# Two groups of indirect DMAs on GpSimd's queue change places in a mixture-of-experts kernel

## The reference

```python
h = layernorm(x).reshape(-1, 128)                 # 2048 tokens
probs = softmax(h @ router_weight.T)              # 8 experts
topk_probs, selected = top_k(probs, 2)            # each token goes to two experts
capacity = ceil(1.25 * 2 * 2048 / 8)              # 640 rows to an expert
expert_inputs = rows of h, gathered per expert    # [8, 640, 128]
pre  = expert_inputs @ ff_pre_act_weight.T        # [8, 640, 512]
gate = expert_inputs @ gate_weight.T
expert_out = (pre * silu(gate)) @ ff_post_act_weight.T
out = x + scatter_add(expert_out * kept_weight)   # back to the tokens' rows
```

## Time and profile before

| what | us |
|---|---|
| median of 3 timed runs (lowest, highest) | 385.89 (384.17, 385.9) |
| span of the profiled execution, first to last instruction | 410.6 |
| PE busy | 305.2 |
| VectorE busy | 290.1 |
| GpSimd busy | 211.5 |
| ScalarE busy | 144.4 |

### The profile page before, as it was taken

One profiled execution on the slowest core, in us unless ns is written; L12 is line 12 of the kernel. 1 busy time (PEld: TensorE's weight loads), 2 busy tenths in 40 slices (PEclk: granted clock), 3 DMA queues, 4 the chain that ended last, 5 costly groups with the idle time before them and its releaser, 6 DMA issues.

```text
span 410.6 us, 5169 instructions
## 1 busy us (share of the span) xinstructions
PE 305.2 (74%) x1465; PEld 212.9 (52%) x1465; DVE 290.1 (71%) x615; ACT 144.4 (35%) x285; POOL 211.5 (52%) x145
## 2 busy tenths in 40 slices
PE   5969996776798669766591866969695959597940
PEld 4635342333344335333261555959594949497940
DVE  5954999999999999999978843646363636362500
ACT  2535963223533353344042003333332323233320
POOL 0632455974455435543714062174848484848664
PEclk9965996887888878988786798978797979798995
DMA  6040024254000000000002011144443333323332
GB/s 186 2 102 0 0 52 102 62 140 164 14 13 0 26 26 0 0 26 26 0 27 77 1 41 26 32 92 76 72 85 59 79 62 86 55 48 43 29 26 25
DMA packets 20756, 20.31 MB, mean 49 GB/s; under 512 B 2624, under 2 KB 14848, under 8 KB 20736
## 3 DMA queue, kind: packets, MB, share of 16 engines
q1 hardware_dynamic: 13184, 14.63, 12.4%
q0 software_dynamic: 7040, 5.25, 10.3%
q10 hardware_dynamic: 512, 0.19, 0.3%
HBM read 10.82 MB, written 5.05 MB: 39 GB/s over the span
## 4 chain that ended last, share of the span: by engine, by line
PE 38%; DVE 25%; issue 13%; another core or an unknown queue 9%; POOL 7%; ACT 4%; DMA 1%; DVEq 1%; POOLq 1%; ACTq 0%
PE psum L1481 10%; DVE ring L518 8%; PE psum L1460 5%; PE psum L1315 5%; DVE ring L509 5%; PE psum L1462 5%; PE psum L1461 4%; POOL ring L1130 4%; PE psum L1298 2%; DVE sm L543 2%; POOL out L1197 2%; DVE xn L457 1%; POOL parts L1119 1%; PE psum L1295 1%
## 5 line engine op out<-in xcount | busy, mean ns | idle before, releaser
L1130 POOL TENSOR_TENSOR ring<-ring,cbc 128x1024 f32<-128x1024 f32 x31 | 74.9, 2416 | 85.7 <-DVE ring L518 85.7
L518 DVE TENSOR_TENSOR_SCAN ring<-ring 128x1024 f32<-128x1024 f32 x32 | 102.6, 3210 | 0.0
L1315 PE MATMUL psum<-ring,cst 128*128 128x512 f32 x128 | 76.4, 729 | 15.4 <-POOL ring L1130 15.3
L1298 PE MATMUL psum<-stack,sel_r 128*128 (+1 forms) x120 | 55.8, 572 | 25.4 <-DVE ring L509 24.7
L1197 POOL DMA_INDIRECT out<-ring,sid x40 | 62.9, 1572 | 16.9 <-issue 11.0
L1180 POOL DMA_INDIRECT ring<-rows,gid x40 | 38.7, 968 | 63.4 <-DVE gid L780 39.5
L817 DVE TENSOR_TENSOR ring<-psum,ring 128x320 f32<-128x320 f32 x64 | 31.4, 491 | 56.0 <-ACT ring L1048 30.6
L1460 PE MATMUL psum<-stack 128*128 128x320 f32 x128 | 47.6, 372 | 27.2 <-issue 16.4
L935 ACT ACTIVATE ring<-psum,nega 128x510 f32<-128x510 f32 x64 | 41.7, 681 | 46.1 <-PE psum L1298 44.4
L1048 ACT ACTIVATE ring<-psum 128x320 f32<-128x320 f32 x64 | 27.9, 438 | 78.7 <-PE psum L1462 50.8
L1298 PEld LDWEIGHTS psum<-stack,sel_r 128*128 128x128 f32 x120 | 25.1, 224 | 53.4 <-DVE ring L509 33.6
(11 more groups left out here) (180 smaller groups left out, 342.4 us busy)
## 6 DMA issues: line engine op xcount, KB each, us to landing
stack<-parts SPq DMA_DIRECT2D x16, 256.0 KB, 3.8
win_s<-in_wg SPq DMA_DIRECT2D x8, 256.0 KB
win_s<-in_w SPq DMA_DIRECT2D x8, 256.0 KB
w_s<-in_w SPq DMA_DIRECT2D x8, 256.0 KB
xt<-in_x SPq DMA_DIRECT2D x4, 256.0 KB, 4.7
out<-xt SPq DMA_DIRECT2D x4, 256.0 KB, 2.3
rows<-xn SPq DMA_DIRECT2D x4, 256.0 KB, 2.3
ring<-rows,gid POOLq DMA_INDIRECT x40
```

Of the source, the lines that this page charges most:

```text
L518: v.tensor_tensor_scan(hh[:, s].rearrange("p a b -> p (a b)"), da[:, s].rearrange("p a b -> p (a b)"), uu[:, s].rearrange("p a b -> p (a b ...
L1130: g.tensor_tensor(hc[:, s], hh[:, s], cb, ALU.mult).then_inc(s_product, 1)
L1298: ins = mm(bank(to + k), sel, stack[:, half, kind, bass.ts(c, CH)], start=True, stop=True)
L1315: ins = mm(bank(YB), wred[:, o:o + D], hc[:, s, k, :], start=(grp == 0), stop=(grp == NG - 1))
```

## The change

In GpSimd's `expert`, the block that waits for the row numbers of expert `e+2` and issues its five gathers moves from ahead of the five scatters of expert `e` to behind them. Nothing is added or removed.

```diff
             def expert(e, b, more=True):
 
-                if more:
-                    gather_ready(e + 2, b)
-                    for q in range(NQ):
-                        gather(b, q)
                 pool.wait_ge(s_scatter_ids, 2 * e + 2)
                 for q in range(NQ):
                     pool.wait_ge(s_weighed, NQ * e + q + 1)
...
                     g.indirect_dma_start(out=out, out_offset=bass.IndirectOffsetOnAxis(ap=sid[:, b, q:q + 1], axis=0),
                                          in_=ye[:, b, q, :], in_offset=None, compute_op=ALU.add
                                          ).then_inc(s_scattered, 16)
+                if more:
+                    gather_ready(e + 2, b)
+                    for q in range(NQ):
+                        gather(b, q)
```

## The result

The kernel after takes 444.85 us in the median of four timed runs (444.15 to 447.76), the kernel before 385.89 (384.17 to 387.4). The ratio is 1.151, with a 95% interval of 1.146 to 1.156: 59 us slower, where 57 were forecast (443.0 us).

A forecast was written before the change was run, and what follows sets the result against it. GpSimd's issuing was taken to bound the timed kernel at 15.8 us a round; the new chain of 25.4 us a round adds 34.5 + 22.6 = 57.1 to 385.9, giving 443.0 us (429 to 450; 8 in 10: 418 to 455).

The forecast's parts named there:

- the 24.7 us: Profiled span of the kernel before, 410.6 us, less its timed median, 385.89; forecast held timed GpSimd lacks 22.6 us of waits.
- the profiled pace: Rival: timed rounds are as long as the profiled ones, so only 34.5 us count: 420 us (407 to 428), chance 0.17.
- The chain: GpSimd and PE work that overlapped becomes one sequence from expert e's first scatter to e+1's: 23.1 to 26.6 us, middle 25.4.
- last issue to its transpose: From the end of the fifth gather's issue on GpSimd to PE's transpose: 2.68 us, with 1.61 as the other end.
- last transpose to the next `up`: On PE, one transpose, two `down` tiles, table, last `down` tile: 3.29 us at full clock, 5.1 at 0.50.
- `up` to the first scatter: From the start of PE's `up` to GpSimd's first scatter: 2.69 us, some 0.7 longer at the low clock.
- The row-number wait: GpSimd's wait before the gathers of expert e+2: taken at nothing behind the scatters, at most 5.1 us.
- The landing: Fifth gather, from the start of its issue to its transpose: 3.63 us by the row, 2.15 by the skill's estimate.
- The clock: PE's granted clock in the burst after waiting for gathers: 1.00 or 0.50, rounds 24.13 or 26.6 us, middle 25.4 taken.
- The low end of 5.1: Last transpose to next `up` at clock 0.50: 3.29 us lengthened by the 1.55 ratio of tile pairs, 2.77 against 1.79.
- The sum: Expert 6's scatters 34.5 us later than profiled, plus 22.6 us of waits: 57.1 on 385.9 gives 443.0 us.
- Issues shorter than their rows: Rival: GpSimd's issues take less time than traced, round 18.0 us, 376 us in all; not slower has chance 0.04.

## Why the prediction was right

**The reading of the long profile.** The choice that the 24.7 us belong to one profiled execution, and that GpSimd's issuing bounds the timed rounds, was argued from a sum. The second profile of the kernel before shows it: no waits, a span of 382.3. Had the profiled pace been taken as real, the forecast would have been 420, too low by 25 us. What delayed that one execution stays open. Its silus waited for matmuls that had been issued, and neither the second profile of before nor the profile after shows such "remote" waits.

**The chain.** The terms of a round, forecast and measured in the six rounds of the trace after:

| term | forecast, us | measured, us |
|---|---|---|
| five scatters | 9.11 | 9.07 to 9.12 |
| gap to the gathers | 0.30 | 0.30 to 0.31 |
| five gathers | 6.06 | 6.05 to 6.07 |
| last issue to its transpose | 2.68 (1.61) | 1.89 to 2.63 |
| last transpose to the next `up` | 3.29 to 5.1 | 4.56 to 5.84 |
| `up` to the first scatter | 2.69 to 3.4 | 2.77 to 2.96 |
| round | 25.4 | 26.0 in the mean |

The row-number wait was costed at nothing, and no gather of the rounds waits for it. The landing was a little quicker than the row taken: 329.63 - 326.79 = 2.84 us from the start of the last gather's issue to its transpose in the round shown, and 3.4 to 3.6 in the others, against 3.63. The Trainium skill ("DMA: Bandwidth & Descriptors", Anatomy of one DMA) led to an estimate of 2.15; the rows decide, and the estimate is low.

**The clock** is the term that was mis-sized. The forecast took the middle between a burst at the full and at the low level, 4.2 us for the stretch from the last transpose to the next `up`. It took 5.2 in the mean: in the round shown nearly all of the burst is at the low level (0.51) behind 11 us with PE busy for 2. The low end of 5.1 was itself too short for such a round (5.7). It came from a ratio of 1.55 for two tiles, read from a pair that began at 0.50 and ended after the clock was back at 1.00; here the pair takes 3.41 against 1.79, 1.9 times as long. Landing and `up` took back some 0.4 us a round. The slow start of the burst is as the Trainium skill ("TensorE: Matmul & The Clock Gate", HAM oscillation) has it, that a burst behind each DMA wait starts slow; by that rule the forecast was 450 us, since it also put the first matmuls of `up` at the low level. They are not: `up` to the first scatter takes 2.77 to 2.96 us.

**The sum.** First scatter of expert 0: forecast 4.3 us earlier than before, 267.1 against 271.40. In the trace after and the second one of before it is 260.07 against 264.22, so 4.15 earlier. Six rounds after: 152.0 forecast, 155.96 measured. The way from expert 0's first scatter to expert 6's before: forecast 113.2 - 22.6 = 90.6, measured 356.45 - 264.22 = 92.2. So -4.15 + 155.96 - 92.2 = 59.6 us, and the spans differ by 442.1 - 382.3 = 59.8. Two errors, of 4.0 us in the rounds after and 1.6 in those before, offset each other and left the forecast 2 us low: the mechanism was right, and part of the closeness is luck.

**The rivals.** The profiled pace fell with the second profile. Issues shorter than their rows fell too: rows of 1.56 and 0.95 us with their gaps add up to 15.8 us a round, and the kernel before runs at 16.0 in its second profile, with GpSimd issuing without a pause.

## What to carry to other kernels

A queue that serves two consumers one behind the other ties them together: before an issue is moved behind a wait, follow what that wait needs back to the moved issue, and if the path closes on itself, the cost is the sum of the loop less what bounded the round before. Here the price was then paid per issue that stood ahead, not once, and could be read off durations that the trace already had. And when a profiled span is longer than the timed median, the profile's waits may not be those of the timed runs; a second profile settled it here.

## What was not expected

The scatters' landing takes longer than their issue and is mostly hidden here. With one scatter ahead of the gathers, 4.53 us passed from the end of the last scatter's issue to the first scatter of the next expert, against an issue of 1.56. In the kernel before it also holds VectorE, which waits for scatters to land before it writes new row numbers (L788), as the waits of the second profile show:

```profile
DVE tk L788 <- DMA out<-ring,sid: 23.1, 6, 5.4
```

That they did not set the rounds is read from GpSimd's having no pause beside them, and from the 4.95 us or more that the weighed tiles were early. Where a round has fewer issues, the landing does show, in the kernel before too. Expert 6 has no gathers ahead of its scatters, and its first scatter waits 2.57 us:

```profile
356.45 1.56 POOL L1197 DMA_INDIRECT out<-ring,sid  x1 [2.57 <-DVE kw L791]
355.67 0.17 DVE L788 SCALAR_TENSOR_TENSOR tk<-tab,cst 128x5 f32<-128x5 f32 x1 [2.62 <-DMA out<-ring,sid]
```

Both rows are of the second profile. The first names L791, but L791 of expert 6 ran at 340.97; VectorE's L788, which waits for the same scatters of expert 5, starts at 355.67, when they have landed.
